# Narrow attention layer of a four-layer kernel: row tiles of 64, separate PSUM rings, and steps of one key tile

## The reference, cut to what matters

```
def _L1_xattn_ref(x, cond, wq, wk, wv, wo, norm_w):
    xn = rmsnorm(x, norm_w)
    q = (xn @ wq).reshape(B, T, N_HEADS, HEAD_DIM)        # 2048 rows, 16 heads of 16
    k = (cond @ wk).reshape(B, S, N_KV_HEADS, HEAD_DIM)   # 1601 rows, 4 heads of 16
    v = (cond @ wv).reshape(B, S, N_KV_HEADS, HEAD_DIM)
    scores = jnp.einsum('btgrd,bsgd->bgrts', qg, k) * scale
    attn = jax.nn.softmax(scores.astype(jnp.float32), axis=-1)
    out = jnp.einsum('bgrts,bsgd->btgrd', attn, v).reshape(B, T, N_HEADS * HEAD_DIM)
    return residual + out @ wo
```

## Time and profile before

| | |
|---|---|
| median of 3 runs | 4587.44 us (4586.96 to 4593.1) |
| the profiled execution | 4585.05 us, span 4583.2 us |
| PE busy | 4489.1 us, 98% |
| DVE busy | 3081.9 us, 67% |
| ACT busy | 2308.6 us, 50% |
| chain that ended last | PE 92%, DVE 5% |
| narrow layer, first maxima tile to the copy of the last values | 1642.6 to 2345.4 us |

### The profile page before, as it was taken

The page is one execution under the profiler, slowest core; times in us unless marked ns, Lnnn a source line. Parts: engine busy times, 40 slices in busy tenths (PEclk is TensorE's granted clock), DMA queues, the critical chain, the costliest instruction groups (busy, mean ns, idle before and its releaser), DMA issues.

```text
span 4583.2 us, 56873 instructions
## 1 busy us (share of the span) xinstructions
PE 4489.1 (98%) x20657; PEld 2837.0 (62%) x20657; DVE 3081.9 (67%) x5037; ACT 2308.6 (50%) x4121; POOL 2826.9 (62%) x1365
## 2 busy tenths in 40 slices
PE   8999999999999979999999999999999999999999
PEld 8888766666666445555556666666656666666664
DVE  4221567777777678778746777777767677777776
ACT  3232455555455436666655554555555545555553
POOL 0000378888888701011136898889885888898886
PEclk9999999999999979999999999999999999999999
DMA  5564922222122021011233221222116212222220
GB/s 169 163 215 145 315 67 50 63 69 68 44 65 51 13 40 16 12 15 16 57 120 101 68 69 44 66 67 61 44 47 220 63 45 60 63 69 60 53 48 29
DMA packets 124633, 349.68 MB, mean 76 GB/s; under 512 B 28085, under 2 KB 46005, under 8 KB 113338
## 3 DMA queue, kind: packets, MB, share of 16 engines
q1 hardware_dynamic: 124352, 346.04, 28.6%
HBM read 191.31 MB, written 120.31 MB: 68 GB/s over the span
## 4 chain that ended last, share of the span: by engine, by line
PE 92%; DVE 5%; issue 1%; DMA 1%; ACT 0%; SPq 0%; POOL 0%; DVEq 0%; ACTq 0%
PE ST L1004 14%; PE SS L985 12%; PE ST L1005 12%; PE OA L1015 12%; PE OB L1015 11%; PE ST L1149 5%; PE OA L1157 4%; PE SS L1135 3%; DVE acc L1600 2%; PE OB L1135 1%; PE SS L1024 1%; PE ST L1080 1%; PE ST L1081 1%; PE SS L1051 1%; PE ST L1082 1%
## 5 line engine op out<-in xcount | busy, mean ns | idle before, releaser
L880 POOL TENSOR_TENSOR acc<-acc,P 128x1024 f32<-128x1024 f32 x912 | 2216.5, 2460 | 298.6 <-DVE acc L1606 285.4
L1340 ACT ACTIVATE P<-ST 128x512 f32<-128x512 f32 (+1 forms) x2496 | 1463.2, 597 | 1260.0 <-PE ST L1005 1128.6
L1579 DVE TENSOR_REDUCE mpart<-SS 128x1 f32<-128x400 f32 (+1 forms) x3072 | 1629.2, 569 | 667.7 <-PE SS L985 591.8
L1004 PE MATMUL ST<-QX,KX 128*128 128x512 f32 (+1 forms) x2496 | 1023.4, 410 | 3.6 <-DMA QS<-mrow 1.7
L985 PE MATMUL SS<-KS,QS 68*128 68x400 f32 (+1 forms) x3072 | 977.0, 352 | 14.9 <-DMA QS<-stq 8.2
L1005 PE MATMUL ST<-QS,KS 69*128 69x512 f32 (+1 forms) x2496 | 989.0, 396 | 0.0
L985 PEld LDWEIGHTS SS<-KS,QS 68*128 68x128 f32 x3072 | 583.6, 190 | 191.2 <-DVE xacc L1630 24.8
L1004 PEld LDWEIGHTS ST<-QX,KX 128*128 128x128 f32 (+1 forms) x2496 | 463.4, 186 | 360.7 <-issue 272.8
L1015 PE MATMUL OA<-P,Vp 128*64 128x512 f32 (+1 forms) x2496 | 658.3, 606 | 0.0
L1015 PE MATMUL OB<-P,Vp 128*64 128x512 f32 (+1 forms) x2496 | 641.3, 592 | 0.0
L1439 ACT ACTIVATE PG<-ST 128x512 f32<-128x512 f32 (+1 forms) x832 | 426.5, 618 | 213.5 <-PE ST L1149 213.3
(11 more groups left out here) (250 smaller groups left out, 4484.2 us busy)
## 6 DMA issues: line engine op xcount, KB each, us to landing
q_parts<-stq SPq DMA_DIRECT2D x96, 512.0 KB, 5.1
QX<-q_parts SPq DMA_DIRECT2D x96, 512.0 KB, 11.2
KX<-k_parts SPq DMA_DIRECT2D x48, 801.0 KB, 9.4
QS<-q_parts SPq DMA_DIRECT2D x45, 512.0 KB
R<-R SPq DMA_DIRECT2D x360, 64.0 KB, 2.0
v_tiles<-sv SPq DMA_DIRECT2D x24, 832.0 KB, 6.7
Vp<-v_tiles SPq DMA_DIRECT2D x24, 832.0 KB, 7.3
k_parts<-skh SPq DMA_DIRECT2D x48, 400.5 KB, 4.7
```

The source lines that it names most:

```text
L880: gp.tensor_tensor(out, out, P[0:k, slot(H, t), q, :], ALU.add).then_inc(pool_a, 1)
L1004: pe.matmul(bank, KX[H % 2][:, t * 128:t * 128 + k], QX[H % 2][:, q], start=True, stop=False)
L1340: act.activation(P[0:k, slot(H, t), j, :], ST[n % 3][0:k, :], ACT.Exp, scale=SCALE).then_inc(act_p, 1)
L1579: dve.tensor_reduce(mpart[H % 2][:, i // len(KCH), c:c + 1], SS[RING_AT["s", H, i] % 3][:, 0:w], AX.X, ALU.max).then_inc(dve_ss, 1)
```

## The change

All of it lies in the narrow layer.

1. The stacked rows go from one block of 112 to two halves, rows 0 to 47 and rows 64 to 111 (`HALF = 64`, `GROWS = 48`): three blocks of 16 rows each, keys (high, high, low), queries (high, low, high); the product of the two low parts is left out. Both halves of `KG` hold the same keys. The queries are divided: the first half holds query blocks 0 and 2, the second blocks 1 and 3. The maxima sit in rows 48 and 112. Each matmul of scores or maxima therefore reads 48 or 49 rows and is placed in a tile of 64 rows by 128 columns of the PE array, at row 0 or at row 64. They are issued in pairs, one in each half.
2. The scores get a fourth bank (`GST = ST + [OA]`), the values go to `OB`, and the ring of everything else has three banks (`SS`) in place of four.
3. A step covers one key tile: 13 steps a head in place of 7, each with 4 scores tiles in two pairs, 2 or 3 pairs of maxima tiles, and the 4 value matmuls of one key tile.
4. The queries of a head are stacked by 6 DMAs in place of 4, the row of maxima by 2 in place of 1, the keys of a group by 6 in place of 4 (24 in place of 16 in all); POOL sets 8 small blocks to one instead of 4, and no longer clears `GQ`.

More of the change, by code:

```diff
@@ L1164, in group_sums @@
                 wait_group_ring(pe, at)
-                pe.matmul(GS[at % 4][:, :], sel[:, :], Oraw[:, h % 2, :], start=True, stop=True).then_inc(gpe_z, 1)
+                pe.matmul(group_bank("z", h, 0)[:, :], sel[:, :], Oraw[:, h % 2, :], start=True, stop=True).then_inc(gpe_z, 1)
             def group_output(rnd, i):
-                at, ct, j = GRING_AT["o", rnd, i], i % CT, i // CT
+                ct, j = i % CT, i // CT
                 if i == 0:
@@ L1431, in group_take_o @@
                 wait(act, gpool_on, 4 * (h - 1))
-                copy(Oraw[:, h % 2, :], OA[:, :]).then_inc(gact_o, 1)
+                copy(Oraw[:, h % 2, :], OB[:, :]).then_inc(gact_o, 1)
             def group_exps(h, t, j):
@@ L1438, in group_exps @@
                 act.wait_ge(gpe_st, n + 1)
[L1439 removed]
+                act.activation(PG[slot(h, t) * JQ + j][0:k, :], GST[n % 4][0:k, :], ACT.Exp, scale=SCALE1).then_inc(gact_p, 1)
             def group_head(h):
[L1442 to L1443 removed]
+                for t in range(KT):
+                    if group_takes_sums(h, t - 1):
                         group_take_z(h - 1)
[L1445 to L1448 removed]
+                    both = group_units(h, t)
+                    for w in range(len(both) // 2):
+                        for on, ts, j in both[2 * w:2 * w + 2]:
+                            group_exps(h + on, ts, j)
+                        if group_q_item(h, t, w) is not None:
+                            group_hi(h // QHEADS + 1, group_q_item(h, t, w))
                 group_take_o(h)
@@ L1464, in group_layer @@
                     group_hi(0, j)
-                for t in PV[0]:
-                    for j in range(JQ):
-                        group_exps(0, t, j)
+                for j in range(JQ):
+                    group_exps(0, 0, j)
                 for h in range(HEADS):
@@ L1750, in group_layer @@
                     group_lo(0, j)
-                for i in range(SUNITS):
+                for i in range(GPAIRS):
                     group_s_max(0, i)
```

97 lines of the change are left out of this document (42 added, 55 removed).

## The result

| | before | after |
|---|---|---|
| median | 4588.72 us (4 runs, 4586.96 to 4593.1) | 4702.74 us (4 runs, 4699.92 to 4714.48) |
| profiled execution | 4585.05 us, span 4583.2 | 4702.11 us, span 4700.5 |
| granted clock, mean | 0.989 | 0.965 |

The change made the kernel 2.56% slower: ratio 1.0256, 95% interval 1.0243 to 1.0269. The forecast was 4646 us, in a range of 4595 to 4705. The direction is right, and the forecast has half of the measured size. Medians and ratios here and in the table of the experiments leave out two executions that were disturbed and ran at a lower clock, 4749.04 us of e3 (the profiled one, so e3 has no clock in the table) and 5532.26 us of e14.

A forecast was written before the change was run, and what follows sets the result against it. It took PE to run at DVE's pace between values, with DVE idle during values. Heads 1 to 13 +51, projections +11, front and head 0 +4, head 14 +1, head 15 -5: +62 on 4585, 4646 us, range 4595 to 4705.

The forecast's parts named there:

- The clock falls: Rival, chance 0.04: granted clock falls to 0.50, 1.7 us more per passage, 320 us if for the whole layer: 4970 us.
- The sum at the full clock: All terms of the narrow layer added, with no fall of the clock: +62 us on 4585, giving 4646 us.
- The 13 passages: Trips to the values and back per head, 7 before: DVE idle 0.79 us each, 10.3 us a head against 7.2.
- The +0.8 us for sums and turned maxima: These 128-row matmuls now sit between 64-row ones and pay extra mode changes: +0.8 us a head.
- Pairs overlap: Paired matmuls run at once: worth nothing between values; the first pair behind values keeps the maxima tile's 0.34 us start.
- The rival of pairs one after the other: Rival, chance 0.13: pairs don't overlap, 0.23 us x 13 = 3 us a head, 4690 us, up to 4710.
- Steps of one key tile and the ring of three: In each steady head, more passages to the values and one ring bank fewer: DVE idles more, +3.1 us a head.
- Last head: Head 15, without maxima tiles: the fourth scores bank lets ACT run nearly through, -5 us.
- The front of the layer: Start of the narrow layer: added DMA issues 1.8 us, maxima row 0.6 us; with head 0, together +4 us.
- Output projections: Output projections between 64-row matmuls in three heads: 9.4 us a head where 6.5 us were, +2.9 us each.
- Query projections: Query projections in head 6, 128-row matmuls now between 64-row ones: about +2 us, within +11 us for all projections.
- The faster rival: Rival, chance 0.10: PE is the bound and pairs free it, 4500 us; milder, change-over costs nothing, about 4575 us.

The follow-up runs named there:

- e3: The changed kernel with three banks for scores and a ring of four for maxima tiles, as before the change; 4664.25 us, ratio 1.0173.
- e14: The changed kernel with scores and maxima tiles reading 64 and 63 rows instead of 49 and 48, added query rows zero; 4648.95 us, ratio 1.0131.
- e1: The kernel before with only the stacking in two halves of 48 rows, its steps, rings and order kept; 4672.96 us, ratio 1.0184.
- e2: The changed kernel with the full-height stacking of before (112 rows), keeping one-tile steps, four scores banks and ring of three; 4661.86 us, ratio 1.0163.
- e10: Same as e2, but with the banks of before: three for scores and a ring of four; 4635.72 us, ratio 1.0105.
- e16: The changed kernel with three scores banks, a ring of four, and matmuls reading 64 and 63 rows a half; 4609.08 us, ratio 1.0043.

## Why the prediction was wrong, point by point

- **The step that failed: "The clock falls", chance 0.04.** The argument against it was "in the last head, where PE computes for 3.5 of 5.43 us, the clock is 1.00". That row was of matmuls over 113 rows; it says nothing of matmuls over 49. The last head of e1 has the same order with 49 rows, has cold stretches, and takes 43.4 us where 32.8 were. The rival was also priced as all or nothing, 320 us. It came for part of the time: 277 - 54 = 223 us more cold, at the 0.35 us of e14, is 78 us. Its price for one passage was about right (1.7 us forecast, 1.57 measured).
- **The sum at the full clock was too high.** 117 us in the profiled executions (4702.11 - 4585.05) less 78 is 39 us, where the forecast had 61. With the prices of 0.30 and 0.41 us for a cold us it is 50 and 26. The two misses have opposite signs; had the clock held, the forecast would have been some 10 to 35 us too long. A head is +2.8 us, not +3.9, which is 14 us of it.
- **Where the head was mis-sized.** The 13 passages after came as reckoned: DVE stands 0.70 us at most of them, in the count by which the earlier trace rows have 0.23 and 0.92 us. The error is in the passages of before. The prediction read one passage of two key tiles (0.92 us) and took it for all six. The six of a head are not alike:

```profile
1853.40 1.54 DVE L1685 TENSOR_REDUCE mpart<-SS 128x1 f32<-128x402 f32 x3 [0.92 <-PE SS L1135]
...
1860.26 0.57 DVE L1685 TENSOR_REDUCE mpart<-OB 128x1 f32<-128x400 f32 x1 [1.94 <-PE OB L1135]
...
1866.24 1.06 DVE L1685 TENSOR_REDUCE mpart<-SS 128x1 f32<-128x402 f32 x2 [1.08 <-PE SS L1135]
...
1872.24 0.57 DVE L1685 TENSOR_REDUCE mpart<-OB 128x1 f32<-128x400 f32 x1 [1.09 <-PE OB L1135]
...
1878.11 0.28 DVE L1696 CAST mrow<-SS 16x128 fp32r<-16x128 f32 x1 [0.71 <-PE SS L1142]
...
1882.02 0.58 DVE L1685 TENSOR_REDUCE mpart<-SS 128x1 f32<-128x402 f32 x1 [1.70 <-PE SS L1135]
```

  With the 0.23 us of the single one the head before has 7.7 us of idle DVE, the head after (1839.98 to 1882.48) 9.8 us: +2.1 us, where the forecast had 3.1 and 0.8. The other 0.6 us of the +2.8 lie outside these waits and are not explained. The +0.8 us for sums and turned maxima isn't there: the passage with the sums stood 1.94 us before, 1.02 above the 0.92, and stands 1.75 after, 1.05 above the 0.70.

```profile
1900.04 2.02 DVE L1729 TENSOR_REDUCE mpart<-SS 128x1 f32<-128x400 f32 x4 [1.75 <-PE SS L1175]
```

- **Pairs overlap: right, and so is their price.** The rival of pairs one after the other (0.13) is refuted by 0.50 us for two scores tiles that start at 1905.72. The prediction gave pairs nothing between values and 0.23 us at the first pair behind them, 3.0 us a head. e2, without pairs, has 2.6 us more in a head than the changed kernel at the full clock, and DVE stands 0.93 us over the values where it stands 0.70 with pairs.
- **Steps of one key tile and the ring of three: right in sign.** e2 has both at full height, and the fourth scores bank: 1.63%, 75 us. e10 splits this into 48 for the steps and 27 for the exchange of a bank.
- **Last head: right, by the bank that was named.** -5.4 us for -5; e2 against e10 shows 6.3 us for the fourth bank.
- **The front of the layer: right only in part.** The first maxima tile starts at 1642.15 (1642.59 before), so the added DMA issues cost nothing, where 1.8 us for the queries' two were reckoned. But head 0 ends at 1745.33, 17.7 us later than before (1727.67), and the clock stays at 0.50 to 1740, not to 1684. The forecast for the front as a whole was +4.
- **Output projections: a little high.** In e14 heads 5 and 9 lie at the full clock and take 51.0 us, 8.5 more than its other heads, where it was 6.5 before: +2.0 us for a forecast of +2.9.
- **Query projections: too low.** Head 6 takes 59.2 us after (1982.03 to 2041.22), some 10 us more than the 48.87 of before; the forecast came to about 6. e2, whose clock stays, has 56.2 there, so most of that isn't the clock.
- **The faster rival (0.10)**: not here. Even e16, with pairs at the full clock and the ring of four, stays 0.43% above the kernel before.

## What to carry to other kernels

Before splitting a contraction into row tiles, look at what sets the pace, and then at the granted clock of the stretches after it, not at the mean of the run: 0.965 for 0.989 hid 277 us at half the clock in a layer of 820 us. If small matmuls bring the clock down, try to let them read more rows, even zeros; here that gave back 54 us of 114 and left the heads at the full clock as long as they were. A waiting time read at one place has to be read at the others of its kind before it is multiplied. A row at one shape is no evidence for the clock at another, and a rival that depends on the clock should be priced for a part of the time, too.
